# A sixteen-sample transformer kernel on one core: the norm of the next sample is finished inside the previous pass, the query and key projections change banks, and the calls of every engine are put in another order

## The reference, cut to what matters

```python
x = L0_attn_x                                  # (16, 512, 256)
h = layernorm(x) * (1 + ca) + sa               # ca, sa, ga ...: six vectors per sample
# attention, 16 heads of 16
k, q, v = h @ Wk.T, h @ Wq.T, h @ Wv.T
k, q = ln(k), ln(q)                            # over the 16 values of a head
attn = softmax(causal(q k^T / 4))
x = x + ga * (attn v @ Wu.T)
h = layernorm(x) * (1 + cb) + sb
# feed-forward
h = silu(h w1) * (h w2)                        # 256 -> 1024
h = gelu(h h1); h = gelu(h h2)                 # 1024 -> 1024, twice
x = x + gb * (h w3)                            # 1024 -> 256
# layer 1
h = layernorm(x) * (1 + ca) + sa
xp, z = split(h @ W_in)                        # 512 and 512
dt = clip(softplus((xp W_xproj)[:64] W_dt + b_dt), 0.001, 0.1)
state = (1 + A dt) * state + B dt xp           # 512 steps, 16 states, per channel
y = (sum_n C_n state_n + D xp) * silu(z)
x = x + ga * (y @ W_out)
h = layernorm(x) * (1 + cb) + sb
x = x + gb * (quantise(h) @ quantise(weight).T + bias)
```

## Time and profile before

| | |
|---|---|
| Median of three executions | 4272.72 us (4272.13 to 4274.93) |
| The profiled execution: its time, its span | 4271.38 us, 4269.6 us |
| PE busy | 3649.2 us, 85% |
| DVE busy | 3540.8 us, 83% |
| ACT, POOL busy | 2423.0 us (57%), 2416.6 us (57%) |
| Mean granted TensorE clock | 0.925 |
| A whole pass, from its first `att_norm` to the next one's | 240.6 to 242.5 us; 248.1 us where the loop turns |

### The profile page before, as it was taken

One profiled execution on the slowest core, in us unless ns is written; L12 is line 12 of the kernel. 1 busy time (PEld: TensorE's weight loads), 2 busy tenths in 40 slices (PEclk: granted clock), 3 DMA queues, 4 the chain that ended last, 5 costly groups with the idle time before them and its releaser, 6 DMA issues. The chain is left out here.

```text
span 4269.6 us, 51341 instructions
## 1 busy us (share of the span) xinstructions
PE 3649.2 (85%) x17261; PEld 2207.8 (52%) x17261; DVE 3540.8 (83%) x3917; ACT 2423.0 (57%) x3413; POOL 2416.6 (57%) x1895
## 2 busy tenths in 40 slices
PE   5688898989999898989998898989989898999523
PEld 3364555646464555647464554647465564646211
DVE  4514888989898998989898998989898898989795
ACT  2334555657566665656655665656666665756432
POOL 0131755648484755749484665848375664848362
PEclk8698999999999999999999999999999999999756
DMA  4630211203030210203030120303021120303000
GB/s 156 242 119 11 80 35 36 84 6 114 1 104 16 70 50 30 90 6 114 1 100 21 50 70 16 104 6 100 15 85 35 42 78 11 109 1 104 0 5 5
DMA packets 69436, 247.79 MB, mean 58 GB/s; under 512 B 9600, under 2 KB 10112, under 8 KB 68736
## 3 DMA queue, kind: packets, MB, share of 16 engines
q1 hardware_dynamic: 66816, 235.28, 16.3%
q10 hardware_dynamic: 2304, 8.39, 0.5%
HBM read 212.19 MB, written 31.46 MB: 57 GB/s over the span
## 5 line engine op out<-in xcount | busy, mean ns | idle before, releaser
L668 POOL TENSOR_TENSOR kept<-kept,hb 128x512 f32<-128x512 f32 x640 | 807.9, 1297 | 74.0 <-DVE hb L1820 74.0
L1811 DVE TENSOR_TENSOR_SCAN hb<-ps,hb 128x512 f32<-128x512 f32 x640 | 746.1, 1205 | 8.8 <-ACT ps L1332 7.0
L881 PE MATMUL ps<-hid_bhi,wring 128*128 128x512 f32 x1536 | 631.4, 411 | 82.9 <-issue 57.2
L881 PE MATMUL ps<-hid_blo,wring 128*128 128x512 f32 x1536 | 622.1, 405 | 0.0
L636 POOL TENSOR_TENSOR kept<-kept,hb 128x1024 f32<-128x1024 f32 x128 | 299.4, 2356 | 529.1 <-DVE hb L1755 425.4
L1332 ACT ACTIVATE ps<-kept,a_neg 128x512 f32<-128x512 f32 x640 | 427.2, 692 | 174.4 <-DVE hb L1811 172.2
L881 PE MATMUL ps<-hid_ahi,wring 128*128 128x512 f32 x1280 | 516.4, 403 | 8.6 <-POOL hid_alo L683 7.5
L881 PE MATMUL ps<-hid_alo,wring 128*128 128x512 f32 x1280 | 504.3, 394 | 0.0
L1498 ACT ACTIVATE room<-ps 128x2048 f32<-128x2048 f32 (+1 forms) x192 | 305.7, 1592 | 322.6 <-PE ps L1086 322.4
L1881 DVE TENSOR_REDUCE room<-ps 128x4 f32<-128x2048 f32 (+3 forms) x256 | 374.9, 1485 | 117.3 <-PE ps L1060 115.8
L621 POOL TENSOR_SCALAR_AFFINE_SELECT room<-room 128x512 f32<-128x512 f32 x256 | 203.8, 810 | 409.1 <-ACT room L1498 408.6
(11 more groups left out here) (188 smaller groups left out, 7465.7 us busy)
## 6 DMA issues: line engine op xcount, KB each, us to landing
wring<-w_hi SPq DMA_DIRECT2D x352, 512.0 KB, 3.3
kept<-in_wffn SPq DMA_DIRECT2D x22, 512.0 KB, 6.1
w_hi<-wring SPq DMA_DIRECT2D x22, 512.0 KB, 6.6
w_lo<-wrest SPq DMA_DIRECT2D x22, 512.0 KB, 5.2
xn<-in_x_fm SPq DMA_DIRECT2D x17, 512.0 KB, 3.4
out_fm<-xc ACTq DMA_DIRECT2D x16, 512.0 KB, 3.1
room<-in_wmod SPq DMA_DIRECT2D x2, 1536.0 KB, 8.1
win<-in_win SPq DMA_DIRECT2D x1, 1024.0 KB, 8.5
```

Of the source, the lines that this page charges most:

```text
L668: pool.tensor_tensor(acc[:, m, :], acc[:, m, :], hb[:, s % 8, :], ALU.add).then_inc(acc_done, 1)
L881: mm = pe.matmul(bank(bk), wring[:, r % 3, at + k * P:at + (k + 1) * P], src[i][:, k, :], start=(k == 0 and i == 0), stop=(k == K - 1 and ...
L1811: dve.tensor_tensor_scan(hb[:, s % 8, :], bank(2 + m % 2), hb[:, s % 8, :], 0.0, ALU.mult, ALU.add).then_inc(scanned, 1)
```

## The change

1. The norm of the next sample gets semaphores of its own (`next_*`), a flag `nxt` in `Pass`, squares in `qk_sq` and a logarithm tile `next_log` in `room`. `next_affine` at the end of the pass takes the place of `att_norm` at the start of the next: it writes in place, into `ln_x`, with a column `m_next` that `pick_next` (a new DVE copy) has picked ahead. `ln_x` is then the input of the projections, so the `pre` norm waits for `v_done` and `qk_done`, and `h_ln` is free.
2. `project` writes banks 6 and 7 in turn instead of 0 to 3, `head_var` writes bank 4 alone, and each of the four tiles has a buffer `qk_rs[i]` of its own.
3. `scores(0, 0)` waits for the first query and key tile in the even version, `scores(1, 0)` for the same in the odd version, `scores(2, 0)` and `scores(3, 0)` for all.
4. The even version moves from DVE (a tensor_scalar) to ACT (an Identity activation).
5. The lists of calls of the four compute engines are in another order throughout.

```diff
-        VAR_BANK = (2, 3, 0, 1)
+        QK_BANK = (6, 7, 6, 7)
...
+            def pick_next():
+                if nxt:
+                    dve.wait_ge(att_in, since(att_in, 0))
...
+                    dve.tensor_copy(m_next[:, :], src.rearrange("p a b -> p (a b)")).then_inc(next_mod, 1)
...
             def next_mean():
-                if ffn:
+                if nxt:
                     pe.wait_ge(x_loaded, since(x_loaded, 16))
-                    pe.wait_ge(gelu_done, since(gelu_done, 4 * HM))
-                    pe_mean(pe, xn, k_next, 6)
+                    if ffn:
+                        pe.wait_ge(gelu_done, since(gelu_done, 4 * (HM - 1) + 2))
...
             def project(i):
                 if att:
-                    pe.wait_ge(att_in, since(att_in, DC))
                     if i == 0:
-                        pe.wait_ge(b_ready, since(b_ready, 0))
-                        pe.wait_ge(b_copied, since(b_copied, 0))
...
+                        pe.wait_ge(att_in, since(att_in, 0))
+                    if i >= 2:
+                        pe.wait_ge(qk_normed, since(qk_normed, i - 1))
...
-                        mm = pe.matmul(bank(i), wqk[:, c, m * P:(m + 1) * P], h_ln[:, c, :], start=(c == 0), stop=(c == DC - 1))
+                        mm = pe.matmul(bank(QK_BANK[i]), wqk[:, c, m * P:(m + 1) * P], ln_x[:, c, :], start=(c == 0), stop=(c == DC - 1))
...
             def head_var(i):
...
-                    pe.matmul(bank(VAR_BANK[i]), head_mat[:, :], qk_sq[:, i % 2, :], start=True, stop=True).then_inc(qk_summed, 1)
+                    if i:
+                        pe.wait_ge(qk_logged, since(qk_logged, i))
...
+                    pe.matmul(bank(4), head_mat[:, :], qk_sq[:, i % 2, :], start=True, stop=True).then_inc(qk_summed, 1)
...
             def normalise(i):
...
-                    dve.tensor_tensor(rs, bank(i), rs, ALU.mult).then_inc(qk_normed, 1)
-                    dve.wait_ge(qk_normed, since(qk_normed, i + 1))
-                    w = 2 * (i % 2)
-                    dve.tensor_scalar((q_ver, k_ver)[i % 2][:, 0, i // 2, :], rs, qkw[:, w:w + 1], qkw[:, w + 1:w + 2],
-                                      ALU.mult, ALU.add).then_inc(ver_even, 1)
+                    dve.tensor_tensor(rs, bank(QK_BANK[i]), rs, ALU.mult).then_inc(qk_normed, 1)
...
             def scores(quad, u):
+                if u == 0:
+                    pe.wait_ge((ver_even, ver_odd)[p], since((ver_even, ver_odd)[p], 2 * c + 2))
                 if quad == 0:
-                    if u == 0:
-                        pe.wait_ge(ver_even, since(ver_even, 4))
-                        pe.wait_ge(ver_odd, since(ver_odd, 4))
...
             def pre_centre():
                 if pre:
                     if att:
-                        dve.wait_ge(att_in, since(att_in, DC))
+                        dve.wait_ge(v_done, since(v_done, 2))
+                        dve.wait_ge(qk_done, since(qk_done, 4))
...
-            def att_norm():
...
+            def next_affine():
+                if nxt:
+                    act.wait_ge(next_norm, since(next_norm, 1))
+                    act.wait_ge(next_mod, since(next_mod, 1))
                     for c in range(DC):
-                        act.activation(h_ln[:, c, :], ln_x[:, c, :], ACT.Identity, bias=m0[:, SA + c:SA + c + 1],
+                        act.activation(ln_x[:, c, :], ln_x[:, c, :], ACT.Identity, bias=m_next[:, SA + c:SA + c + 1],
...
+            def even_version(i):
+                if att:
+                    w = 2 * (i % 2)
+                    act.wait_ge(qk_normed, since(qk_normed, i + 1))
+                    act.wait_ge(mid_done, max(0, since(mid_done, -DC)))
+                    act.activation((q_ver, k_ver)[i % 2][:, 0, i // 2, :], qk_rs[i], ACT.Identity, bias=qkw[:, w + 1:w + 2],
+                                   scale=qkw[:, w:w + 1]).then_inc(ver_even, 1)
```

644 lines of the change are left out of this document (342 added, 302 removed).

## The result

The changed kernel took 4254.83 us, the median of six executions (4243.86 to 4258.66); the kernel before, beside it, 4273.83 (4269.98 to 4276.56). The ratio is 0.9952, interval 0.9940 to 0.9964: faster by 19 us, or 1.3 us in each of the 15 passes with a body. The forecast was 4213, 4.0 us a pass. The time lies in the range of 4130 to 4285; the size was missed by a factor of three.

What follows compares the result with a forecast made beforehand. PE and DVE were taken to share the bound, with DVE followed through its short waits. 3.7 + 0.3 = 4.0 us over 15 passes gave 4213 us; own range 3 to 6 us a pass (4183 to 4228), 8-in-10 range 4130 to 4285.

Steps and rivals of the forecast that it cites:

- The sum: Whole pass: 3.7 + 0.3 = 4.0 us saved in each of 15 passes, 60 us in all.
- 3.7: At head_in(0, 0): starts at 2102.8 instead of 2106.50 with the same work done, a lead of 3.7 us.
- 0.3: End of the attention part: ffn_scale comes out at 2155.8 against 2156.05, 0.3 us.
- Feed-forward, priced at 0 with a bound of 5 us: Feed-forward part: same matmuls, DVE idles 5.0 us in 100; left as it is, bound 5 us either way.
- Through the gate: First scores to head_in(0, 0): lead falls to 0.1 us at shift_q(1), then returns to 3.7 at head_in(0, 0).
- rival 4: Second exponential late behind gate_in and in_proj at PE's lower clock: 2 us a pass slower, 4303; chance 0.17.
- Even versions, 0.60 us each: Four even versions moved from DVE to ACT: 0.60 us each, 2.4 us a pass off DVE.
- the flush rule: Waits between chained DVE operations add nothing: four versions worth 1.8 us, not 2.4, forecast 8 us later; not adopted.
- The clock at the boundary: Pass boundary: a 2.4 us PE idle piece might lower the clock, costing up to 1.6 us per following group.
- The softplus wait: Before head_in(0, 0): softplus still waited for, 2.6 us, as the 2.75 before.
- The wait for make_u: Before head_in(0, 0): make_u still waited for, 1.2 us for 0.93.
- the second: At the gate: lead lost for good, only work taken off DVE stays, 15 x 1.7 = 25 us, 4247; chance 0.14.

Runs made afterwards that it cites:

- The runs with one half of it (4335 and 4287): Changed kernel with the old feed-forward order but the early norm, 4334.96 us; kernel before with the new feed-forward order but the late norm, 4287.18 us.
- The split of x_proj: Changed kernel with the first two of x_proj's four terms moved on PE behind row_sums(0), some 4 us earlier: 4224.98 us, ratio 0.9885 to before.
- The four kernels behind the split: x_proj halves plus: earlier spread; scores(3, 0), find_max(3, 0) earlier; the first plus scores_turned(0, 2), exp_probs(0, 2) earlier; all together: 4253.74, 4253.83, 4255.95, 4273.59 us.
- the one with more matmuls: Kernel with x_proj in two halves, plus five unused matmuls on PE behind scores(3, 1) and turn_sums(1): 4250.84 us, ratio 0.9946 to before.

## Why the prediction was wrong

**The sum.** The step that failed is "3.7 + 0.3 = 4.0 us a pass". 3.7 was the lead of head_in(0, 0) over before and 0.3 that of ffn_scale, some 50 us later in the same pass. The same work stands ahead of ffn_scale in both orders (DVE's instructions from the pick to it differ by the four even versions and the copy of pick_next alone), so 0.3 was the whole lead there and not something to add to the earlier one. By its own rows the walk said: the attention part gives 0.3, and the feed-forward part, priced at 0, decides. The runs bear out this reading. As means of the twelve passes, head_in(0, 0) stands at 88.3 us after the pick in both kernels: the 3.7 measured 0. ffn_scale stands at 139.03, before at 138.92: no lead either. Up to it DVE has 114.0 us of work for 118.0 and idles 25.0 for 21.0, so that the waits took back all that was taken off. From ffn_scale to the next pick it is 101.5 us for 103.0, with the same work and 2.8 us of idle time for 4.3: 1.4. Together that is 1.3 us a pass, as are the measured 19 us over 15.

**Feed-forward, priced at 0 with a bound of 5 us.** This is the term that was mis-sized. The numbers for it were there: on the page of the kernel before, the group of times_c (L1820) waits 26.7 us for spreads, 1.7 a pass, and there are 0.39 us before the last scale. I looked at the idle share of 100 us and at the matmuls, which are the same, and not at where the new order puts the spreads. The runs with one half of it (4335 and 4287) show that the new order and the earlier norm are one edit.

**Through the gate.** Up to shift_q(1) the walk held: the first row maximum at 12.9 (12.6), exp_probs(0, 1) at 44.55 (44.4), the wait before tail_in of state 2 at 2.69 (2.5), shift_q(1) at 52.25 (51.8). Behind it head_in(0, 0) came at 88.4 and not 84.1. Of these 4.3 us, 3.1 are x_proj at the lower clock; before, the clock was 1.00 at this place in every ordinary pass, and x_proj took 3.65. This is rival 4's mechanism at another place: I looked for it in gate_in and in_proj, big tiles one after the other, which ran at full clock, and behind PE's pause at the boundary. The Trainium skill, page "TensorE: Matmul & The Clock Gate", section "Why this matters for your kernels", warns of long idle gaps, longer ones than the 2.4 us that the prediction had at the boundary, so it did not speak against the move as the prediction took it to. Where PE paused for 5.21 us the trace agrees. But here the clock was at 0.59 over 5 us in which PE is shown busy for all 5.00, behind matmuls of 32 rows and of 4 columns, and with 6.46 us busy in the 7 ahead (2065 to 2072) and no pause over 0.33. The split of x_proj, which puts 2 us of full tiles among them, shows it from the other side. That it did so by those tiles and not by shifting the rest is likely, not shown: in_proj(3), moved to nearly the same place, did not.

**Even versions, 0.60 us each.** Right on DVE: 0.61 us from a normalise to what follows, for 1.19. So the 0.14 us beyond the operation were real: by the flush rule that the prediction set against them (the Trainium skill, "VectorE: DVE Perf Modes", "The DRAIN you can't avoid") the step would have become 0.73. As time of the kernel it has no price of its own: +3.4 us a pass undone in the new order, and alone in the old order a loss of 1.1.

**The clock at the boundary.** The pause was 1.55 us, not 2.4, and the clock stayed at 1.00 for the next 20.

**The rest.** DVE's work fell to 212.9 and not 215, partly since other small operations became shorter (the three copies of the pick 659 ns on average for 984). A pass was 239.2 us at best and 241.7 otherwise, for the 238 forecast. The softplus wait that I put at 2.6 us was 2.13; the 2.75 that I set beside it is in its row a wait of out_add for out_proj (L1002), not for softplus. The wait for make_u that I put at 1.2 us was gone. Of the rivals, the second comes nearest in size (4247), but not by its mechanism: the work came off DVE ahead of ffn_scale, where nothing was gained. The measured 1.3 us lie outside the forecast's own 3 to 6.

**What stays open.** What makes the clock fall in one pass and not in the next, with all instructions the same before it, is not settled. The two passes above do differ a little at the first fall: x_proj starts 64.38 us after the pick and takes 5.67 in the one, 64.62 and 5.42 in the other, so the lower level begins and ends at slightly different points of their work. The second fall decides over 2.5 us a pass, more than the change gave. The four kernels behind the split and the one with more matmuls each shifted it, and none as expected.
